# A four-layer attention and expert kernel: layer 0 sends q and k through DRAM, ScalarE divides its probabilities, and the clearing of the expert slots moves

## The reference, cut to what matters

```python
x = x + jnp.tanh(g_xattn[0]) * _L0_xattn_ref(_layernorm(x, axis=-1), ctx_4096, ctx_4096, pos_BxS2, ...)
x = x + jnp.tanh(g_ffn[0]) * _L0_ffn_ref(_layernorm(x, axis=-1), ...)
...
# layer 0's attention: 32 query heads, 8 key heads of 128
k = k * cos + _rotate_half(k) * sin          # and the same for q
scores = jnp.einsum('bhqd,bhkd->bhqk', q, k) / jnp.sqrt(jnp.float32(D))
scores = jnp.where(mask == 0, jnp.float32(-1000000000.0), scores)
attn = jax.nn.softmax(scores, axis=-1)
x = jnp.einsum('bhqk,bhkd->bhqd', attn, v)
return x.transpose(0, 2, 1, 3).reshape(nb, q_len, H * D) @ Wo
```

## Time and profile before

| | us |
|---|---|
| median of 3 runs | 2588.79 |
| lowest, highest | 2585.55, 2595.55 |
| the profiled execution, its own time | 2584.26 |
| its span, first to last instruction | 2582.5 |
| mean granted TensorE clock | 0.963 |

### The profile page before, as it was taken

One profiled execution on the slowest core, in us unless ns is written; L12 is line 12 of the kernel. 1 busy time (PEld: TensorE's weight loads), 2 busy tenths in 40 slices (PEclk: granted clock), 3 DMA queues, 4 the chain that ended last, 5 costly groups with the idle time before them and its releaser, 6 DMA issues. The chain is left out here.

```text
span 2582.5 us, 40807 instructions
## 1 busy us (share of the span) xinstructions
PE 2343.2 (91%) x12485; PEld 1966.3 (76%) x12485; DVE 1860.8 (72%) x3505; ACT 1231.7 (48%) x3610; POOL 1484.4 (57%) x1572
## 2 busy tenths in 40 slices
PE   5899999998889999999887888899779999999977
PEld 4788888887777888888766776676568888888753
DVE  4677777777778888887775776563377888888762
ACT  2444445444235666665533555223235666666421
POOL 4566656654226777776535666422446777776443
PEclk9999999999999999999899999899889999999989
DMA  3234444443225555555410000149614555554354
GB/s 107 77 115 144 156 161 150 163 152 115 74 82 183 178 178 172 179 175 174 143 58 17 1 1 27 65 152 364 235 58 151 175 178 178 175 175 157 122 197 153
DMA packets 261421, 356.26 MB, mean 138 GB/s; under 512 B 19313, under 2 KB 167409, under 8 KB 258266
## 3 DMA queue, kind: packets, MB, share of 16 engines
q1 hardware_dynamic: 245472, 304.51, 36.5%
q0 software_dynamic: 10224, 42.03, 4.7%
q10 hardware_dynamic: 5514, 7.11, 0.9%
HBM read 252.88 MB, written 134.45 MB: 150 GB/s over the span
## 5 line engine op out<-in xcount | busy, mean ns | idle before, releaser
L1389 ACT ACTIVATE W<-S,nmx 128x128 f32<-128x128 f32 x768 | 299.8, 396 | 123.7 <-DVE nmx L1717 118.4
L2306 POOL TENSOR_TENSOR W<-W,rden 128x512 f32<-128x512 f32 x192 | 200.2, 1043 | 148.2 <-DVE rden L1722 147.6
L2312 POOL TENSOR_TENSOR pT_l<-W,pT_h 128x512 fp32r<-128x512 f32 x184 | 239.0, 1299 | 70.5 <-ACT pT_h L1210 69.7
L1732 DVE STREAM_TRANSPOSE S<-W 128x512 f32<-128x512 f32 x184 | 130.7, 710 | 177.1 <-POOL W L2306 176.2
L2242 POOL TENSOR_TENSOR ring_l<-raw,ring_h 128x512 fp32r<-128x512 f32 x166 | 215.7, 1302 | 63.0 <-ACT ring_h L1210 62.8
L911 PE MATMUL B_s<-kT,qT_h 128*128 128x256 f32 x768 | 197.5, 334 | 35.6 <-DVE xnT_l L1532 14.7
L854 PE MATMUL B_out<-ring_h,oT_h 128*128 128x512 f32 x516 | 209.9, 407 | 7.0 <-DVE kT L1532 3.6
L854 PE MATMUL B_out<-ring_l,oT_h 128*128 128x512 f32 x516 | 204.9, 397 | 0.0
L854 PE MATMUL B_out<-ring_h,oT_l 128*128 128x512 f32 x516 | 204.1, 396 | 0.0
L911 PEld LDWEIGHTS B_s<-kT,qT_h 128*128 128x128 f32 x768 | 149.0, 194 | 58.0 <-issue 46.3
L2266 POOL TENSOR_TENSOR qT_l<-q_in,qT_h 128x512 fp32r<-128x512 f32 x104 | 134.9, 1297 | 72.7 <-ACT qT_h L1210 71.6
(11 more groups left out here) (504 smaller groups left out, 7739.7 us busy)
## 6 DMA issues: line engine op xcount, KB each, us to landing
raw<-in_pieces SPq DMA_DIRECT2D x270, 256.0 KB
between_p<-S SPq DMA_DIRECT2D x184, 256.0 KB, 2.7
W<-between_p SPq DMA_DIRECT2D x184, 256.0 KB, 2.9
between_q<-xn SPq DMA_DIRECT2D x104, 320.0 KB, 3.4
q_in<-between_q SPq DMA_DIRECT2D x104, 320.0 KB, 3.1
slots_x<-in_zero SPq DMA_DIRECT2D x32, 1030.0 KB, 7.1
raw<-in_experts SPq DMA_DIRECT2D x16, 768.0 KB, 7.0
w<-in_experts SPq DMA_DIRECT2D x8, 1024.0 KB, 16.8
```

The source lines that it names most:

```text
L1389: t = act.activation(probs_r, scores_r, ACT.Exp, bias=nmx[:, k, r:r + 1], accum_out=den[:, k, r:r + 1])
L1732: dve.transpose(blocks_first(S[:, k, :]), W[:, k, :].rearrange("p (r j q) -> p r j q", r=R, q=BLOCK)).then_inc(*blocks_made.now((layer, u)))
L2306: pool.tensor_tensor(W3, W3, rden[:, k, :].unsqueeze(2).to_broadcast([P, R, P]), ALU.mult).then_inc(*probs.now((layer, u)))
L2312: pool.tensor_tensor(heads_first(pT[1][:, :]), by_block(W[:, k, :]), heads_first(f32(pT[0][:, :])), ALU.subtract).then_inc(*p_split.now((l ...
```

## The change

Four things change in the order and in who does what.

1. Units 8 to 59 of layer 0 join `TURNED_BY_DMA`: their q and k go through DRAM, TensorE no longer transposes them, and GpSimd (not VectorE as in layers 1 and 3) makes the low part of k.
2. For these units ScalarE divides the probabilities, with four activations of 128x128, each with its own scale per partition; GpSimd's product is dropped.
3. `split_p` of these units stands at place 70.3 of its step, behind v's copy and the rotation of the unit projected there; before it stood at 60, ahead of them.
4. The clears of the expert slots start with layer 2's small heads (`self.first[2]`) in place of step 16.

The waits of a few parts follow (`k_low`, `probs_act`, the first two normalised blocks of `ffn0`, the first low-rank copy). The diff, cut:

```diff
-TURNED_BY_DMA = {(layer, u) for layer in (1, 3) for u in range(NB, G * NB - 4)}
+TURNED_BY_DMA = {(layer, u) for layer in (0, 1, 3) for u in range(NB, G * NB - 4)}
...
-                self.at(i + 4, 45, "split_p", layer, u)
+                self.at(i + 4, 70.3 if layer == 0 else 45, "split_p", layer, u)
...
-            self.at(i + lag, 10.5 if KINDS[layer] == "norm" else 0,
+            self.at(i + lag, 10.5 if KINDS[layer] == "norm" or (layer, u + lag - 1) in TURNED_BY_DMA else 0,
                     "add_out", layer, u)
...
-                self.at(16 + 2 * n, 47, "clear_slots", n)
+                self.at(self.first[2] + 2 * n, 47, "clear_slots", n)
...
+            def normalise_p(layer, u):          # ScalarE
+                if layer == 0 and (layer, u) in TURNED_BY_DMA:
+                    k = unit(layer, u)[3]
+                    act.wait_ge(*rden_done.of((layer, u)))
+                    for r in range(R):
+                        t = copy(W[:, k, cols(r)], W[:, k, cols(r)], rden[:, k, r:r + 1])
+                    t.then_inc(*probs_act.now((layer, u)))
...
             def turn_low(b):
                 act.wait_ge(*low_turned.of(b))
+                if b == 0:
+                    act.wait_ge(*q_low.of((0, LAST_BY_DMA)))
+                    act.wait_ge(*k_low.of((0, LAST_BY_DMA)))
...
-                if stage in ("ffn1", "ffn3") and b < 2:
+                if stage in ("ffn0", "ffn1", "ffn3") and b < 2:
...
             def split_k(layer, u):              # VectorE
                 kind = KINDS[layer]
+                if layer == 0 and (layer, u) in TURNED_BY_DMA:
+                    return
...
+            def split_k(layer, u):              # GpSimd
+                if layer == 0 and (layer, u) in TURNED_BY_DMA:
+                    pool.wait_ge(*kT_hi.of((layer, u)))
+                    pool.tensor_tensor(keys_by_part(kT[1]), keys_in, keys_by_part(f32(kT[0])), ALU.subtract
+                                       ).then_inc(*k_low.now((layer, u)))
+
             def normalise_p(layer, u):          # GpSimd
+                if layer == 0 and (layer, u) in TURNED_BY_DMA:
+                    return
```

More of the change, by code:

```diff
@@ L654, in qk_read, with k_split, probs_made @@
             return (q_blocks if (layer, u) in TURNED_BY_DMA else qk_turned).of((layer, u))
+        def k_split(layer, u):
+            return (k_low if layer == 0 and (layer, u) in TURNED_BY_DMA else kT_lo).of((layer, u))
+        def probs_made(layer, u):
+            return (probs_act if layer == 0 and (layer, u) in TURNED_BY_DMA else probs).of((layer, u))
         def q_split(layer, u):
@@ L670, in build @@
                                 "pT_hi", "oT_hi"))
-        rows_hi, q_blocks, q_low, low_masked, k_scaled = (signal(n) for n in ("rows_hi", "q_blocks", "q_low", "low_masked", "k_scaled"))
+        rows_hi, q_blocks, q_low, low_masked, k_scaled, k_low, probs_act = (
+            signal(n) for n in ("rows_hi", "q_blocks", "q_low", "low_masked", "k_scaled", "k_low", "probs_act"))
         q_stored, q_loaded = ([signal(f"{n}{k}", 16) for k in range(2)] for n in ("q_stored", "q_loaded"))
@@ L907, in scores @@
                 pe.wait_ge(*q_split(layer, u))
-                pe.wait_ge(*kT_lo.of((layer, u)))
+                pe.wait_ge(*k_split(layer, u))
                 bank_free("sc", "kT")
@@ L1520, in scalar_program @@
                      "load_x": load_x, "late_constants": late_constants, "make_gates": make_gates, "make_constants": make_constants, "ln_turn": ln_turn,
-                     "split": split, "project": project, "turn_q": turn_q, "split_k": split_k, "split_q": split_q, "scores": scores, "exp": exp, "turn_p": turn_p, "split_p": split_p, "times_v": times_v, "low": low,
+                     "split": split, "project": project, "turn_q": turn_q, "split_k": split_k, "split_q": split_q, "scores": scores, "exp": exp, "probs": normalise_p, "turn_p": turn_p, "split_p": split_p, "times_v": times_v, "low": low,
                      "turn_low": turn_low, "route2": route2, "weigh2": weigh2, "turn2": turn2, "load_rows2": load_rows2, "expand2": expand2,
@@ L1730, in blocks_p @@
                 k = unit(layer, u)[3]
-                dve.wait_ge(*probs.of((layer, u)))
+                dve.wait_ge(*probs_made(layer, u))
                 dve.transpose(blocks_first(S[:, k, :]), W[:, k, :].rearrange("p (r j q) -> p r j q", r=R, q=BLOCK)
@@ L2404, in pool_program @@
             prologue()
-            parts = {"rope": rope, "ln_stats": ln_stats, "split": split, "project": project, "split_q": split_q, "probs": normalise_p, "split_p": split_p,
+            parts = {"rope": rope, "ln_stats": ln_stats, "split": split, "project": project, "split_k": split_k, "split_q": split_q, "probs": normalise_p, "split_p": split_p,
                      "turn_q2": turn_q2, "group_v2": group_v2, "sum2": sum2, "scatter2": scatter2,
@@ L2470, in load_q @@
                     sync.wait_ge(*q_low.of((layer, u - 1)))
-                    sync.wait_ge(*kT_lo.of((layer, u - 1)))
+                    sync.wait_ge(*k_split(layer, u - 1))
                 elif layer == 1:
```

## The result

| | before | after |
|---|---|---|
| median, us | 2590.06 (4 runs) | 2666.24 (4 runs, 2664.04 to 2667.48) |
| profiled span, us | 2582.5 | 2663.8 |
| mean granted clock | 0.963 | 0.963 |

The changed kernel takes 1.0285 of the time before (95% interval 1.0267 to 1.0304): 76 us slower by the medians. The two profiled executions lie 2665.58 - 2584.26 = 81 us apart. The forecast was 2658 us, the range 2630 to 2708.

What follows compares the result with a forecast made beforehand. TensorE bounded layer 0 before; afterwards two cross-engine loops would, mean step 10.41 us against 9.05. 65 - 1 + 5 = +69 us on the profiled 2584.26 gives 2653; the median lies 4.5 higher: 2658 us, range 2630 to 2708.

Steps and rivals of the forecast that it cites:

- The wait and its place: Layer 0: TensorE stands at times_v waiting for GpSimd's pT_l, 1.53 us in every step.
- First loop: Layer 0: projection, v's copy, rotation on VectorE and GpSimd, pT_l, times_v, projection; 10.19 us per step.
- Second loop: Layer 0: times_v, oT_h, exponentials, ScalarE's division (1.14 us), sq, rotation, pT_l; 10.04 us, 10.54 with a weight piece.
- The dear rival: ScalarE's division costs 0.531 us per activation, 2.12 for four; mean step 11.33 us, total 2702 us; chance 0.12.
- the estimate from the Trainium skill: ScalarE's division: 0.41 us per activation, 1.62 for four; mean step 10.83 us, result 2678 us.
- Five steps in eight: Layer 0: a weight piece stands in ScalarE's order in 5 of 8 steps: 10.54 us there, 10.19 otherwise, mean 10.41.
- How many steps: Layer 0: 48 of 52 steps go from 9.05 to 10.41 us, +65 us; steps 9 to 11 save 1 us.
- The end of layer 0: Turning units 60 to 63 later in the step: within 2 us; nothing counted for projections 57, 58, 62, 63.
- q and k through DRAM: Layer 0: stores and loads of 3.4 and 3.1 us cost 0 while the step is 10.2 us.
- The clears: Beside the small heads they delay loads of ffn2's first weights: +5 us, bounds 0 and 14; no gain in layer 0.
- layer 1's rate: Rival: TensorE stays the bound and layer 0 runs at layer 1's 8.61 us per step; 2571 us; chance 0.05.
- The clock rival: The granted clock as a rival, no size of its own given, taken in by the range; chance 0.07.

Runs made afterwards that it cites:

- Undoing one number: Changed kernel with layer 0's split_p put back to place 45, ahead of v's copy and the rotation: 2587.29 us, ratio 1.0015.
- the fast version: Changed kernel with split_p at 45 and layer 0's maximum ahead of the 32x32 turn of q and k: 2579.4 us, ratio 0.9975.
- the kernel with two pieces: Changed kernel with GpSimd making pT_l of layer 0's units 8 to 59 in two instructions of 128x256: 2673.20 us, ratio 1.0336.
- with four: Changed kernel with GpSimd making pT_l of layer 0's units 8 to 59 in four instructions of 128x128: 2695.74 us, ratio 1.0426.

## Why the prediction was right, point by point

**The wait and its place**: as forecast, TensorE at `times_v`, waiting for `pT_l`. Undoing one number takes it all away. That 1.57 us stand against a forecast of 1.53 is partly luck: the forecast's sums give 1.53 in the shorter steps and 1.88 in the longer, where the trace has 1.35 and 1.67. The sums count from where the next matmul would start, the trace from the end of the last one, 0.16 us later (0.39 us long, 0.23 from start to start).

**First loop**, forecast 10.19 us: the steps without a weight piece are 10.1 to 10.2.

**Second loop**, forecast 10.54 us: measured 10.50 (310.27 - 299.77). `times_v` to division 3.90 against 4.02; division to sq 1.95 against 1.82; sq to `pT_l` 3.33 against 3.37; `pT_l` and release 1.32 against 1.33. So two terms were off by 0.12 and 0.13 us and cancelled. The four activations took 1.28 us, not 1.14. The dear rival's 2.12 was too dear, and so was 1.62, the estimate from the Trainium skill. But that one left out of its sum what the same page ("ScalarE: Activation LUTs", section "What ACT_TABLE_LOAD costs") says beside its measured times: neighbouring ACTIVATEs overlap by about 93 ns. With one operand per partition and three overlaps the page gives 4 x 0.387 - 3 x 0.093 = 1.27 us (estimate), and the trace's 1.28 agrees; one activation lasts 0.391 us there. The loop doesn't hang on ScalarE: with GpSimd dividing most steps are the same, 10.2 and 10.5 us, one in eight 10.3. There its product of 1.06 us is shorter, but starts late, behind the split of a weight piece.

**Five steps in eight**: seen exactly; mean 10.38 against 10.41.

**How many steps**: +62 us from the first to the 58th x addition, against +65 and -1. Right.

**The end of layer 0**: here a term was mis-sized. The prediction has "within 2 us" for it, and "I count nothing there" for four steps that were long before; two of those four lost nothing, and the last six steps together lost 6.5 us. There VectorE's order puts the low parts of q and k, the masks and the maximum between v's copy and the rotation, and a split queued behind the rotation is delayed with it. After, at the end of layer 0:

```profile
680.62 0.27 ACT L1217 ACTIVATE v_h<-B_qkv 128x128 fp32r<-128x128 f32 x1
...
683.63 0.81 DVE L1654 TENSOR_TENSOR sq<-B_qkv,tables 128x640 f32<-128x640 f32 x1
...
688.26 0.79 PE L938 MATMUL B_three<-pT_h,v_h 128*128 128x512 f32 x1 [4.49 <-POOL pT_l L2340]
```

From v's copy to sq it is 3.0 us, in the steady steps 0.7 (304.94 to 305.62). The kernel before had nearly as much there (617.12 to 619.92), but its `times_v` did not wait for the rotation. A step that is already long for another reason is not immune to a new wait: both may lie in the same chain.

**q and k through DRAM**: cost 0 held; TensorE never waits for `qT_l` in these steps.

**The clears**: +5 forecast, 4.4 between the ratios, which isn't clear of noise. 26 clears did go out in one run and kept the DMA engines full for over 80 us, 3.2 us each at 324 GB/s, but the small heads took as long without them (288.3 and 288.2 us). ScalarE's longest wait for a weight piece at their end was 3.3 us, against 3.9 before. So no run shows a cost of this term, and its agreement with the 4.4 is no evidence for it. What the move is good for was not seen either. The prediction said that layer 0 "gains nothing" by it; with steps under 9 us it gains 34 us.

**The rivals**: layer 1's rate needed the split ahead of the rotation, as argued; with that it came near (8.86 us against 8.61), and the clears' rows show one thing that it also needs. The clock rival did not occur; its neighbours show how close it was.

**The sum**: 69 forecast, 76 by the medians, 81 between the two profiled executions. Layer 0's attention is 70 of the 81, against 64: the end of layer 0 was left out. The other 11 lie behind it, where the forecast had 5 for the clears. The profile with the clears in layer 0 has the 2 us in the small heads and 4.9 in the expert part too, so these aren't the clears beside the small heads; what they are, and the rest, stays open. That the total came near has this luck in it.

## What to carry to other kernels

Before an instruction is moved in one engine's in-order queue, follow what it is moved behind back to its source: if that source is the engine which waits for the moved instruction's result, a loop is closed, and its length, not any engine's busy time, is the new step. Add such loops up term by term from one timeline; here two sums were right within 0.05 us, one of them with errors that cancelled. Test background transfers on the fast version as well as on the slow one: a step with slack hides what they cost.

## What the runs showed of the hardware that was not expected

The clock: with stops of 1.35 and 1.67 us, one per step of 10.2 or 10.5 us, TensorE's granted clock stayed 1.00 from 200 to 600 us. With stops of 1.49 and 1.82 us it fell to 0.50, the level of 1.2 GHz, 4 times in these 400 us; with 1.78 and 2.10 us 10 times; and in the kernel before with the split moved, with stops of 2.26 and, six times, 3.38 us, 19 times, six of them for twice as long, at the long stops. One single fall takes away 1.7 us of full clock (0.29 + 0.50 + 0.50 + 0.41, in the windows shown). The falls of single length made their step 1.3 us longer in the kernel with two pieces, 1.2 to 1.6 with four, 1.5 in the one made from the kernel before: less than 1.7, for the next stop is shorter by some of it (1.49 after 1.81 at the falls with two pieces). So here the loss came in whole portions, and a little more stop brought more of them. The Trainium skill, "TensorE: Matmul & The Clock Gate", section "What's actually happening", says that the chip watches TensorE's activity on a clock of its own that doesn't start with the kernel; falls after some stops and not after others of the same length agree with that, but no run here moved the stops against it.

Small instructions side by side: on GpSimd one difference of 128x128 (k's low part) takes 0.52 us, four in a row (`pT_l` in four) 1.70 us, 0.46 each with an overlap, and one of 128x512 1.26 us. Four activations of 128x128 with a scale per partition take 1.28 us on ScalarE, 0.391 each with an overlap of 0.09. A row of four is cheaper than four times one.
